# Selective scan with a shared feed-forward block, then eight experts: the low part of the turned x is made in PSUM, and the copies out of PSUM move to ScalarE

## The reference, cut to what matters

```python
x = L0_attn_x                                     # (1, 4096, 512)
x = x + layernorm(scan_layer(layernorm(x)))       # gives x1
x = x + layernorm(moe(layernorm(x)))              # gives the output

# scan_layer: 512 channels, 16 states each, 4096 steps in time
dt = softplus((x @ W_x)[..., :64] @ W_dt + b_dt)
h  = exp(dt * A) * h + (dt * x) * B_t             # per channel and state
y  = sum over states of h * C_t,  + x * D_skip

# moe: a shared part for all tokens, and two of eight experts per token
sh  = gelu(xt @ sw1 + sb1) @ sw2 + sb2            # 512 -> 2048 -> 512
sh  = sh + gelu(xt @ swd) @ swu                   # 512 -> 32 -> 512
out = experts(xt) + 0.2 * sh
```

## Time and profile before

| | us |
|---|---|
| median of three timed runs | 3348.82 (3348.02 to 3348.97) |
| profiled execution, its own time | 3348.7 |
| span of the profile (first to last instruction) | 3346.7 |
| TensorE, VectorE, ScalarE, GpSimd busy | 3087.1, 1819.5, 1633.8, 1380.8 |

### The profile page before, as it was taken

One profiled execution on the slowest core, in us unless ns is written; L12 is line 12 of the kernel. 1 busy time (PEld: TensorE's weight loads), 2 busy tenths in 40 slices (PEclk: granted clock), 3 DMA queues, 4 the chain that ended last, 5 costly groups with the idle time before them and its releaser, 6 DMA issues.

```text
span 3346.7 us, 42962 instructions
## 1 busy us (share of the span) xinstructions
PE 3087.1 (92%) x15139; PEld 2531.1 (76%) x15139; DVE 1819.5 (54%) x2476; ACT 1633.8 (49%) x2978; POOL 1380.8 (41%) x1367
## 2 busy tenths in 40 slices
PE   6455799988999899999999999999999999999997
PEld 3244677877777777788888888888888888888886
DVE  7799899999999992631332322322313313313345
ACT  7655676766766764542432433423423324324343
POOL 2297898988988884120121022111111111210224
PEclk9655899999999999999999999999999999999999
DMA  8969879697886956820320422312303204204355
GB/s 260 299 189 242 217 220 242 217 262 191 236 229 205 268 162 197 272 79 10 109 59 14 119 38 51 101 23 70 85 17 89 70 13 107 58 13 119 72 187 161
DMA packets 273447, 466.30 MB, mean 139 GB/s; under 512 B 30817, under 2 KB 102193, under 8 KB 273234
## 3 DMA queue, kind: packets, MB, share of 16 engines
q1 hardware_dynamic: 200400, 264.91, 27.4%
q0 software_dynamic: 66720, 189.87, 21.3%
q10 hardware_dynamic: 6114, 8.79, 0.7%
HBM read 366.33 MB, written 97.16 MB: 138 GB/s over the span
## 4 chain that ended last, share of the span: by engine, by line
PE 55%; DVE 2%; issue 1%; ACT 1%; DMA 1%; POOLq 0%; POOL 0%; DVEq 0%; SPq 0%; ACTq 0%
PE c_psH L2067 28%; PE c_psY L2108 26%; PE c_psT L2058 1%; DMA raw<-in_w 1%; PE c_psY L2104 1%; DVE yst L1771 0%; DVE hl L1791 0%; ACT h L1524 0%; DVE hl L1796 0%; PE c_psT L2167 0%; DVE hh L1790 0%; ACT h L1526 0%; ACT hh L1528 0%; DVE hh L1793 0%; DVE d_sum L2004 0%
## 5 line engine op out<-in xcount | busy, mean ns | idle before, releaser
L1796 DVE TENSOR_TENSOR hl<-h,hh 128x512 fp32r<-128x512 f32 (+1 forms) x400 | 242.9, 607 | 1182.3 <-ACT hh L1528 1181.9
L1526 ACT ACTIVATE h<-c_psH,biases 128x512 f32<-128x512 f32 (+1 forms) x400 | 248.3, 621 | 1043.3 <-PE c_psH L2067 1031.3
L919 POOL TENSOR_TENSOR u<-dtxs,Bt 128x512 f32<-128x512 f32 x512 | 661.2, 1315 | 48.8 <-DVE b_psA L812 20.8
L812 DVE TENSOR_TENSOR_SCAN b_psA<-b_psA,b_few,u 128x512 f32<-128x512 f32 x473 | 606.9, 1283 | 39.7 <-ACT b_psA L666 34.5
L2108 PE MATMUL c_psY<-W2h,hh 128*128 128x512 f32 x1344 | 534.5, 398 | 1.7 <-DVE hl L1796 1.1
L2108 PE MATMUL c_psY<-W2l,hh 128*128 128x512 f32 x1344 | 525.0, 391 | 0.0
L2108 PE MATMUL c_psY<-W2h,hl 128*128 128x512 f32 x1344 | 523.9, 390 | 0.0
L1604 POOL DMA_INDIRECT xrow<-xt_d,slot_lists x80 | 84.7, 1059 | 1049.9 <-PE c_psT L2058 600.3
L1038 PE MATMUL b_psY<-ident,pr 128*128 128x128 f32 x2048 | 330.3, 302 | 127.3 <-DVE pr L819 91.0
L1038 PEld LDWEIGHTS b_psY<-ident,pr 128*128 128x128 f32 x2048 | 266.9, 155 | 197.0 <-DVE pr L819 122.2
L1079 PE MATMUL b_psH<-Xh,w 128*128 128x512 f32 x896 | 321.2, 411 | 31.7 <-ACT hb L711 26.5
(11 more groups left out here) (271 smaller groups left out, 5727.6 us busy)
## 6 DMA issues: line engine op xcount, KB each, us to landing
w<-ws_d POOLq DMA_DIRECT2D x224, 512.0 KB, 6.5
raw<-in_w SPq DMA_DIRECT2D x256, 256.0 KB, 2.8
Bt<-bc_d SPq DMA_DIRECT2D x64, 512.0 KB, 12.3
Ct<-bc_d SPq DMA_DIRECT2D x64, 512.0 KB, 20.7
xn<-in_x SPq DMA_DIRECT2D x8, 1024.0 KB, 8.1
xT_d<-xnT SPq DMA_DIRECT2D x8, 1024.0 KB, 13.4
dt_d<-a_dt SPq DMA_DIRECT2D x8, 1024.0 KB, 9.1
dtx_d<-a_dx SPq DMA_DIRECT2D x8, 1024.0 KB, 9.3
```

Source lines behind the costliest of these rows:

```text
L812: nc.vector.tensor_tensor_scan(a[:, :], a[:, :], u[g % U_RING][:, :], carry[:, k:k + 1], ALU.mult, ALU.add).then_inc(s_h, 1)
L919: nc.gpsimd.tensor_tensor(u[g % U_RING][:, :], dtx[s % 2][:, :], Bt[n // TG][:, n % TG, :], ALU.mult)\
L1526: nc.scalar.activation(h32[:, 0:n * P], psH[j % 2][:, 0:n * P], ACT.Gelu, bias=b1[:, j - 1:j])
L1796: nc.vector.tensor_tensor(hl[j % 2][a], h32[a], hh[j % 2][a].bitcast(F32), ALU.subtract)\
```

## The change

- `x_lo` moves. TensorE now turns the tile with the accumulation left open (start at the first of four transposes, no stop). After ScalarE has written `Xh`, TensorE adds a product of minus identity with Xh to the same bank (`take_hi`, X_REST_AT), which leaves the remainder there, and ScalarE copies it to `Xl`. So a tile goes TensorE, ScalarE, TensorE, ScalarE.
- `shared_out` moves from VectorE to ScalarE and only scales by 0.2.
- The bias sb2 is added by two more rows of the low-rank product: hh0 gets two rows of ones, L2 the high and the low part of sb2. The 128-row load of sb2, its scaling and its tile go; a 2-row load, a memset, three small operations of VectorE and one of ScalarE (minus identity) come, all once.
- The tables of units are new throughout, as the diff shows. Among others the last burst of Gelu moves from 93 to 92 (k = 29 to 28), LOW_HI_AT from 56 to 52, LOW_LO_AT from 58 to 55, the first DOWN_AT from 56 to 57, OUT_AT from 118 and 119 to 119 and 120, STATS_AT from 3 to 4, NORM_AT and RESIDUAL_AT one or two units earlier, SKIP_AT from 2 to 4.

```diff
-T_AT = (24, 30, 32, 34)
-X_HI_AT = (27, 30, 33, 37)
-X_LO_AT = (31, 33, 35, 39)
-UP_AT = (38, 40, 44, 46, 47, 52, 54, 56, 61, 63, 66, 70, 73, 75, 79, 81, 86)
-UP2_AT = (38, 41, 44, 47, 47, 53, 54, 56, 62, 63, 66, 71, 73, 77, 79, 82, 86)
-OUT_OF_UP_AT = (40, 43, 46, 48, 50, 54, 57, 60, 63, 66, 69, 74, 76, 79, 82, 86, 89)
-BURST_AT = (52, 65, 78, 93)
-HI_AT = (53, 58, 70, 76, 86, 88, 94, 102)
-LO_AT = (54, 55, 61, 62, 72, 72, 77, 80, 87, 87, 93, 94, 98, 102, 103, 104)
-LOW_HI_AT = 56
-LOW_LO_AT = 58
-DOWN_AT = (56, 59, 63, 69, 71, 74, 78, 79, 84, 87, 89, 94, 96, 98, 103, 106, 113)
-DOWN2_AT = (56, 59, 64, 70, 72, 75, 78, 81, 84, 87, 90, 95, 96, 98, 106, 108, 114)
-OUT_AT = (118, 118, 119, 119)
+L3B = L3 + 2
+T_AT = (23, 29, 34, 37)
+X_HI_AT = (27, 32, 36, 38)
+X_REST_AT = (25, 33, 35, 39)
+X_LO_AT = (29, 33, 37, 39)
+UP_AT = (40, 42, 43, 47, 47, 51, 54, 58, 60, 63, 67, 68, 73, 75, 79, 82, 86)
+UP2_AT = (40, 42, 43, 47, 47, 51, 54, 58, 60, 65, 67, 70, 73, 75, 79, 82, 86)
+OUT_OF_UP_AT = (42, 44, 46, 49, 51, 54, 57, 60, 62, 67, 69, 73, 76, 80, 83, 86, 90)
+BURST_AT = (52, 65, 78, 92)
+HI_AT = (53, 60, 70, 77, 84, 87, 94, 102)
+LO_AT = (53, 55, 60, 61, 72, 73, 79, 81, 88, 88, 92, 94, 97, 98, 104, 106)
+LOW_HI_AT = 52
+LOW_LO_AT = 55
+DOWN_AT = (57, 58, 62, 68, 72, 75, 77, 80, 83, 88, 89, 92, 97, 98, 102, 104, 112)
+DOWN2_AT = (57, 59, 63, 68, 72, 78, 79, 80, 83, 88, 90, 93, 97, 98, 105, 113, 114)
+OUT_AT = (119, 119, 120, 120)
...
-STATS_AT = 3
+STATS_AT = 4
...
-NORM_AT = (6, 7, 8, 9)
-RESIDUAL_AT = (9, 9)
+NORM_AT = (4, 6, 7, 8)
+RESIDUAL_AT = (8, 8)
...
-X1_NORM_AT = (19, 25, 31, 34)
-XT_STORE_AT = (23, 26, 38, 43)
+X1_NORM_AT = (19, 24, 31, 34)
+XT_STORE_AT = (22, 23, 30, 43)
...
-W2_AGAIN = 4
+W2_AGAIN = 3
...
-SKIP_AT = 2
+SKIP_AT = 4
...
+            def x_lo(b, t):
+                act.wait_ge(s_rest, b * BT + t + 1)
+                nc.scalar.copy(Xl[:, :, t * P:(t + 1) * P], psH[:, :].rearrange("p (a b) -> p a b", a=DT))\
+                    .then_inc(s_xlo, 1)
...
+            def shared_out(b, t):
+                if b < FB - 1:
+                    act.wait_ge(s_mm2, (b + 1) * J)
+                else:
+                    act.wait_ge(s_tile, t + 1)
+                after(act, s_sh[t], b * 16)
+                if t >= 2:
+                    act.wait_ge(s_T, min(b + 2, FB + 1) * BT)
+                    act.wait_ge(s_xt[t - 2], min(b + 2, FB + 1) * (BT // 2) * 16)
+                nc.scalar.mul(yst[t][:, :], psS[t][:, :], SHARE).then_inc(s_yev, 1)
...
-            def x_lo(b, t):
-                dve.wait_ge(s_xhi, b * BT + t + 1)
-                cols = slice(t * P, (t + 1) * P)
-                nc.vector.tensor_tensor(Xl[:, :, cols], psH[:, :].rearrange("p (a b) -> p a b", a=DT),
-                                        Xh[:, :, cols].bitcast(F32), ALU.subtract).then_inc(s_xlo, 1)
...
-                nc.vector.scalar_tensor_tensor(yst[t][:, :], psS[t][:, :], SHARE, b2bc[:, :], ALU.mult, ALU.add)\
-                    .then_inc(s_yev, 1)
...
                 for d in range(DT):
-                    last = nc.tensor.transpose(psH[:, d * P:(d + 1) * P], xn[t % 2][:, d * P:(d + 1) * P], ident[:, :])
+                    last = nc.tensor.matmul(psH[:, d * P:(d + 1) * P], xn[t % 2][:, d * P:(d + 1) * P], ident[:, :],
+                                            start=(d == 0), stop=False, is_transpose=True, skip_group_check=True)
                 last.then_inc(s_T, 1)
+
+            def take_hi(b, t):
+                pe.wait_ge(s_xhi, b * BT + t + 1)
+                pe.wait_ge(s_minus, 1)
+                nc.tensor.matmul(psH[:, :].rearrange("p (a b) -> p a b", a=DT), minus[:, :],
+                                 Xh[:, :, t * P:(t + 1) * P], start=False, stop=True, skip_group_check=True)\
+                    .then_inc(s_rest, 1)
```

More of the change, by code:

```diff
@@ L429, in mix @@
         (Xh, Xl), (L1h, L1l), L2 = const["X"], const["L1"], const["L2"]
+        minus = sb("minus_ident", [P, P], F32R)
         hh, hl = sb("hhs", [P, HH_RING, CH], F32R), sb("hls", [P, HH_RING, CH], F32R)
-        g0, hh0 = sb("g0", [P, CH]), sb("b_low_h", [L3, CH], F32R)
-        b2bc = sb("sb2bc", [P, D])
+        g0, hh0 = sb("g0", [P, CH]), sb("b_low_h", [L3B, CH], F32R)
         yst = two("ysh", [P, D]) + xn
@@ L724, in low_rank_hi @@
                 after(act, s_mm2, (b - 1) * J + 1)
-                nc.scalar.copy(hh0[:, :], g0[0:L3, :]).then_inc(s_h0a, 1)
+                nc.scalar.copy(hh0[0:L3, :], g0[0:L3, :]).then_inc(s_h0a, 1)
             def h_hi(b, j):
@@ L756, in static_hi @@
                 nc.scalar.copy(L2[:, :], wu_raw).then_inc(s_lhi, 1)
+                nc.scalar.mul(minus[:, :], ident[:, :], -1.0).then_inc(s_minus, 1)
             for g in range(END):
@@ L783, in _ @@
                     for t in range(BT):
+                        if due(b, X_LO_AT[t]) == g:
+                            x_lo(b, t)
                         if due(b, X_HI_AT[t]) == g:
@@ L788, in _ @@
                 for b in blocks(g):
+                    for t in range(BT):
+                        if due(b, OUT_AT[t]) == g:
+                            shared_out(b, t)
                     for j in range(1, J):
@@ L851, in low_rank_lo @@
                     .then_inc(s_h0, 1)
-            def shared_out(b, t):
-                if b < FB - 1:
-                    dve.wait_ge(s_mm2, (b + 1) * J)
-                else:
-                    dve.wait_ge(s_tile, t + 1)
-                dve.wait_ge(s_b02, 1)
-                after(dve, s_sh[t], b * 16)
-                if t >= 2:
-                    dve.wait_ge(s_T, min(b + 2, FB + 1) * BT)
-                    dve.wait_ge(s_xt[t - 2], min(b + 2, FB + 1) * (BT // 2) * 16)
-                nc.vector.scalar_tensor_tensor(yst[t][:, :], psS[t][:, :], SHARE, b2bc[:, :], ALU.mult, ALU.add)\
-                    .then_inc(s_yev, 1)
             def static_lo():
-                dve.wait_ge(s_stat, 5 * 16)
+                dve.wait_ge(s_stat, 6 * 16)
                 dve.wait_ge(s_lhi, 3)
@@ L876, in static_lo @@
                                         ALU.subtract).then_inc(s_l2, 1)
+                two_rows = slice(L3, L3B)
+                nc.vector.tensor_tensor(bias_low, wu_raw[two_rows, :], L2[two_rows, :].bitcast(F32),
+                                        ALU.subtract).then_inc(s_blow, 1)
+                dve.wait_ge(s_blow, 1)
+                nc.vector.tensor_scalar(bias_low, bias_low, ident[two_rows, L3 + 1:L3 + 2], None, ALU.mult)\
+                    .then_inc(s_blow, 1)
+                dve.wait_ge(s_blow, 2)
+                nc.vector.scalar_tensor_tensor(L2[two_rows, :], L2[two_rows, :].bitcast(F32), ident[two_rows, L3:L3 + 1],
+                                               bias_low, ALU.mult, ALU.add).then_inc(s_l2, 1)
             for g in range(END):
@@ L881, in _ @@
                     static_lo()
-                for b in turned(g):
-                    for t in range(BT):
-                        if due(b, X_LO_AT[t]) == g:
-                            x_lo(b, t)
                 for b in blocks(g):
-                    for t in range(BT):
-                        if due(b, OUT_AT[t]) == g:
-                            shared_out(b, t)
                     if due(b, LOW_LO_AT) == g:
@@ L1095, in down @@
                 if j == 0:
+                    pe.wait_ge(s_one, 1)
                     for t in tiles:
-                        last = nc.tensor.matmul(psS[t][:, :], hh0[:, t * P:(t + 1) * P], L2[:, :], start=True, stop=False)
+                        last = nc.tensor.matmul(psS[t][:, :], hh0[0:L3B, t * P:(t + 1) * P], L2[0:L3B, :],
+                                                start=True, stop=False)
                 else:
@@ L2103, in down @@
                                 pe.wait_ge(s_yev, at["t0"] - (2 if at["k"] == 1 else 4) + min(t, 1 if at["k"] == 1 else 3) + 1)
-                            last = nc.tensor.matmul(psY[t][:, :], hh[0][0:L3, c], L2[:, :], start=True, stop=False)
+                            last = nc.tensor.matmul(psY[t][:, :], hh[0][0:L3, c], L2[0:L3, :], start=True, stop=False)
                             continue
```

24 lines of the change are left out of this document (13 added, 11 removed).

## The result

The changed kernel takes 3366.34 us (median of 5 runs, 3363.31 to 3367.68), the kernel before 3348.97 beside it (5 runs, 3348.02 to 3353.44): a ratio of 1.004, 95% interval 1.0028 to 1.0051 (the two medians alone would give 1.005). The forecast was 3332 with a range of 3316 to 3350. The time and the direction were wrong: the kernel is slower by 0.4 per cent, which is small but clear of the noise.

What follows compares the result with a forecast made beforehand. VectorE was taken to pace the mixing part (134.50 busy of a 142.9 us block), TensorE's floor close behind at 135. Terms -21.6 (six blocks of 3.6), -2.5, +4 and +3 gave -17.1, so 3332 us, range 3316 to 3350.

Steps and rivals of the forecast that it cites:

- what gives part back: Block boundary: time saved in units 52 to 58 may become waits for late step sizes; 0.8 us a block lost.
- the other units: Residual, statistics, norm and skip load moved by one or two units: operations stay the same, counted at nothing.
- Low part off VectorE: Four VectorE operations a block move to ScalarE: gain 2.2 us a block, bounds 1.9 and 2.8; 2.5 in block 1.
- Shared results and low-rank subtraction: Shared results leave VectorE, subtraction moves before the scan awaiting the first burst: gain 2.2 us a block, bounds 0.8 and 3.6.
- GpSimd's wait absorbed by the wait for step sizes: Moved units: GpSimd may wait for statistics, about 2 us of its lead, absorbed by its 2.6 us step-size wait.
- Tail: After the last scan: four new products and a longer tile chain on gapless TensorE add 3 us, bounds 0.9 and 5.
- Start: Kernel start: three one-time VectorE operations on two rows add 4 us, between 2 and 7.7.
- B: Blocks: TensorE, loads or GpSimd take VectorE's place, a block gains only 1.0 us, 3348 us; chance 0.17.
- C: Units 33 and 39: ScalarE waits in order for TensorE's product, VectorE stalls 3.5 us twice a block, 3374 us; chance 0.11.

Runs made afterwards that it cites:

- h5: Kernel before with SKIP_AT 4, bias rows, and low part by minus-identity product and ScalarE copy, shared results on VectorE: ratio 1.006.
- e3: Kernel before with SKIP_AT 4 instead of 2, nothing else: 3342.89 us, ratio 0.9948.
- f1: Changed kernel with the shared results written by VectorE again, as a multiplication: ratio 1.0036.
- h4: Kernel before with SKIP_AT 4, bias rows and shared results on ScalarE (OUT_AT 119, 119, 120, 120), low part still on VectorE: ratio 0.9967.
- j3: h4 with LOW_HI_AT 56 to 52, LOW_LO_AT 58 to 55, and first DOWN_AT and DOWN2_AT 56 to 57: ratio 0.9953.
- f4: Changed kernel with the unit entries of up 2, up 3, up 5 and the second half of down 15 put back as before: ratio 1.0.
- h6: h1 with statistics, norms and residual loads back in the units of the kernel before: ratio 1.0006.
- e1: Changed kernel with SKIP_AT back from 4 to 2, nothing else: 3382.18 us, ratio 1.0058.
- f2: Changed kernel with the low part made by VectorE's subtraction again, minus-identity products and ScalarE's copies of it gone: ratio 1.0192.
- h1: f4 with up 8 also back in units 61 and 62, its hidden out in 63: ratio 1.0014.
- k1: Changed kernel with the next skip row's load issued by GpSimd in unit 9 of a pass, not SyncE in unit 5: 3377.38 us, ratio 1.005.
- j6: j3 with shared results 0 and 1 stored in units 145 and 146 instead of 120 and 121: 3327.53 us, ratio 0.9937.
- e4: All edits of the change with the unit tables of the kernel before, only tile 0's low part moved from 31 to 30: 3398.26 us, ratio 1.0104.

## Why the prediction was wrong

The step that failed is the one on what gives part back. It saw the tables, the late step sizes and a DMA share of 82%, and bounded the loss by "0 and all 2.2", since VectorE showed no wait for loads. Measured, about 8 us came into units 1 to 22, more than both gains. That premise was read from one block: over blocks 2 to 7 the kernel before already waits four times for a C table. The average of 82% hid a stretch of 68 us with a share of 1, in which 4.5 us less work of VectorE shortened nothing. An engine that doesn't wait for the transfers can be just in step with them. The second step that failed is the one on the other units, counted at nothing: it carries most of the loss against the kernel before.

- *Low part off VectorE*, 2.2 forecast: 1.9 came (units 31 to 39; in block 1, 2.5 forecast, the block is 1.7 shorter), and the wait of unit 31 is 2.48 where 2.5 was worked out. But it came by the new units: in the old ones the same move costs 3.3 us there (h5 against e3, units 31 to 49).
- *Shared results and low-rank subtraction*, 2.2 forecast: 3.1 came. By f1 the shared results are worth about 1 of it and by h4 none; the low-rank units bring the rest (j3: 3.0). The subtraction took 0.68 us in its new unit, where I had carried over 2.58, and TensorE's wait of 3.2 for it is gone as forecast. By j3 next to nothing of this gain survives the boundary.
- *Other units*, counted at nothing. With the entries of f4, up 8 and the norms put back (h6) the ratio falls from 1.004 to 1.0006, about 0.3 per cent. The new tables set up and down products closer together ahead of the boundary. TensorE ends the last skip product of a block 8.9 us behind VectorE (4.0 in e3), and more weights land in the full stretch. The skip's own move, counted at nothing too, was worth a gain of half a per cent alone (e3) and of about 0.2 in the changed kernel (e1 against it, with intervals that overlap), so it is not what made the change slower.
- *GpSimd's wait absorbed by the wait for step sizes*: it did the reverse. Late step sizes hold its list 7.5 us in block 5, its inverse comes late, ScalarE's norm waits 3.8 for it and unit 22 pays 3.1.
- *Tail*, 3 forecast (0.9 to 5): 5.2. With the low part back on VectorE (f2) it is 2.5 shorter, so about half belongs to the chain of a tile (in the old units more: 74.2 us in h5, 69.9 in e3). The 0.3 us of signalling in that term was an estimate; the traces show 0.04 from TensorE's modelled end to ScalarE's start. In e3 and h4, which have neither the products nor the new tables, it is already 1.3 to 1.4 longer than before.
- *Start*, 4 forecast: the first block ends 2.3 later.

Of the rivals, B named the mechanism (something takes VectorE's place), but gave it a floor of a gain of 1.0 a block; it had no way to end below zero. C, ScalarE waiting in order for the product, needed a lag that the new units avoid: no such wait shows in block 5. It is what h5 shows with the old units.

Settled: the gains arrive on VectorE, and the boundary takes them back wherever the load's issue or TensorE's products were put (f4, h1, h6, k1, j3), while better places there win back most of the loss (h6). Not settled: that the extra 1.5 MB in the stretch is the whole reason for the 3.8 us. No run takes transfers out of the stretch itself in the changed kernel and leaves all else, and j6 did not lower its bytes. TensorE's added work there is a rival of the same size. f4 and h1 take it back (333 and 326 matmuls for 350 in the changed kernel and 327 before, means of six stretches) and the stretch still takes 71.1 and 70.5 us, with 18.3 and 18.4 MB; so it is not the whole reason either, but the two were never moved apart. And e4 shows that it is not the only way to lose: its stretch takes 71.3 us with 17.9 MB, there VectorE waits for ScalarE.

## What to carry to other kernels

Cut the span by what the DMA queues do, not only by blocks: where their share is 1, expect that an engine's gain there can come back as a wait, and price it low until a run shows otherwise. When hand-written issue times change, list which transfers they release and in which stretch these land. A cheap single edit inside a large change (here the skip's place) should be priced alone, since it may be worth as much as the whole.

## What the runs showed of the hardware

- The low-rank subtraction (32 rows of 512) takes 0.68 us in unit 55, in every block of the changed kernel, f1 and j3, but in unit 58 2.58 to 2.81 in six of seven blocks before, 3.38 in e3 and 2.87 in h4. Looking at what runs beside it, VectorE's and GpSimd's timeline of e3:

```profile
957.75 3.38 DVE L850 TENSOR_TENSOR b_low_h<-g,b_low_h 32x512 fp32r<-32x512 f32 x1
...
959.01 1.27 POOL L919 TENSOR_TENSOR u<-dtxs,Bt 128x512 f32<-128x512 f32 x1
...
960.82 1.45 POOL L919 TENSOR_TENSOR u<-dtxs,Bt 128x512 f32<-128x512 f32 x1
```

  The long ones run beside GpSimd's products of two tensors, the short ones beside a GpSimd that is idle there (968.62 in the changed kernel). Over all 20 traces this is 140 rows: the 108 that overlap products of GpSimd by under 0.2 us take 0.68 to 0.69, the two that overlap 0.29 and 0.34 us take 0.84 and 0.89, the 30 that overlap over 1.4 us take 2.58 to 4.40. VectorE's scans (1.28) and products (0.69), which read one tile from PSUM, take the same beside GpSimd's products as without. The subtraction and GpSimd's product each read two tiles from SBUF. That they get in each other's way is what these rows suggest; no run moved one of them alone.
- Issuing itself can be slow: in the changed kernel three tables took SyncE 12.55 us from 990.79 on, a single one 0.36 at 811.88. The DMA share does not tell the two apart (1.07 in that time, 0.96 in the 4 us around the single one), but the number of SyncE's own transfers that had not landed does: with at most one, the 15 table loads from 406 to 1290 us took 0.36 to 0.37 each, with seven or more, 28 loads took 0.89 to 6.53, 2.6 in the median. A C table took 19.2 us from issue to landing in the median of the whole run and 22.7 from 938 to 1028 us, weights from GpSimd's queue 6.3 and 11.0.
- With a DMA share of about 1 the stretches shown move 247 to 271 GB/s, in four kernels; pieces of 15 us inside them move up to 292.
